# A new hand-written order of the operations on four engines, two merged GpSimd operations and one tile in bf16

## What is computed

```python
xn = _layernorm(x)                       # each row of 128
# branch 1: a complex decaying filter along the 1024 rows, as an FFT convolution
filt = phazor[None, :] ** t * phazor_init[None, :]
conv = ifft(fft(filt, 2 * length) * fft(xn, 2 * length))[:, :length]
y = (conv + last_conv * phazor ** (t + 1)) * gate     # the real part is kept
# branch 2: a gated feed-forward layer in blockwise FP4 (blocks of 16)
gate = fp4_linear(xn, w_gate)            # 128 -> 352
up   = fp4_linear(xn, w_up)              # 128 -> 352
out2 = fp4_linear(silu(gate) * up, w_down)            # 352 -> 128
# fp4_quant_dequant: scale = max|block| / 6, round x / scale to 0, .5, 1, 1.5, 2, 3, 4, 6, times scale
```

## Time and profile before

| | |
|---|---|
| median of 3 runs | 137.35 us (136.39, 139.78, 137.35) |
| the profiled execution | 136.12 us, of which 134.2 us are the span of the instructions |
| busy | DVE 120.5 us (90%), PE 111.9 (83%), POOL 111.0 (83%), ACT 98.9 (74%) |
| mean granted TensorE clock | 0.949 |

### The profile page before, as it was taken

The page is one execution under the profiler, slowest core; times in us unless marked ns, Lnnn a source line. Parts: engine busy times, 40 slices in busy tenths (PEclk is TensorE's granted clock), DMA queues, the critical chain, the costliest instruction groups (busy, mean ns, idle before and its releaser), DMA issues.

```text
span 134.2 us, 2145 instructions
## 1 busy us (share of the span) xinstructions
PE 111.9 (83%) x641; PEld 84.4 (63%) x641; DVE 120.5 (90%) x215; ACT 98.9 (74%) x223; POOL 111.0 (83%) x130
## 2 busy tenths in 40 slices
PE   3603789869377998899899999999999999997993
PEld 3501154536244867677787879686968877787872
DVE  0889999999999999979999999999999999999850
ACT  3869966699983799579897988569776647744541
POOL 4668996999699989999999999999999944982440
PEclk9975799986986999999999999999999999999999
DMA  4990000000000000200020001002000200020111
GB/s 122 280 379 16 0 2 0 0 5 0 0 0 0 5 0 0 78 0 5 0 78 0 0 33 55 0 0 78 0 0 0 83 0 0 0 78 0 67 58 39
DMA packets 2891, 4.90 MB, mean 37 GB/s; under 512 B 448, under 2 KB 832, under 8 KB 2880
## 3 DMA queue, kind: packets, MB, share of 16 engines
q1 hardware_dynamic: 2736, 4.77, 10.4%
q10 hardware_dynamic: 144, 0.00, 0.1%
HBM read 2.67 MB, written 2.10 MB: 36 GB/s over the span
## 4 chain that ended last, share of the span: by engine, by line
POOL 43%; DVE 21%; issue 18%; PE 7%; ACT 6%; DMA 2%; POOLq 1%; DVEq 0%; ACTq 0%
POOL hq L472 9%; POOL y_im L459 6%; POOL y_re L459 6%; POOL u_im L444 5%; POOL u_re L444 5%; POOL xt L416 5%; POOL xt L411 5%; DVE bn L988 4%; POOL xv L406 2%; DMA par<-params_in 2%; ACT xn L629 2%; PE ps_u L853 2%; DVE ps_u L1095 2%; DVE ps_u L1064 1%; DVE ps_u L1060 1%
## 5 line engine op out<-in xcount | busy, mean ns | idle before, releaser
L844 PE MATMUL ps_g<-wg_T,xq_T 128*128 128x352 f32 x64 | 26.8, 502 | 7.3 <-ACT silu L661 5.0
L472 POOL TENSOR_TENSOR hq<-hn,den 128x704 f32<-128x704 bf16 x15 | 20.8, 1390 | 4.3 <-DVE hn L1102 4.3
L904 PE MATMUL ps_o<-wd_T,hq_T 128*128 128x128 f32 x174 | 24.2, 275 | 0.0
L853 PE MATMUL ps_u<-wu_T,xq_T 128*128 128x352 f32 x64 | 23.6, 490 | 0.1
L904 PEld LDWEIGHTS ps_o<-wd_T,hq_T 128*128 128x128 f32 x174 | 22.1, 194 | 0.0
L661 ACT ACTIVATE silu<-ps_g 128x352 f32<-128x352 f32 x32 | 14.8, 461 | 8.4 <-PE ps_g L844 8.1
L844 PEld LDWEIGHTS ps_g<-wg_T,xq_T 128*128 128x128 f32 x64 | 10.3, 193 | 13.2 <-ACT silu L661 8.2
L671 ACT ACTIVATE big<-ps_u 128x704 bf16<-128x704 f32 (+1 forms) x17 | 12.2, 725 | 7.4 <-DVE ps_u L1090 7.4
L667 ACT COPY hq_T<-ps_h 128x384 f32<-128x384 f32 x31 | 14.8, 479 | 3.3 <-PE ps_h L880 3.1
L1095 DVE SCALAR_TENSOR_TENSOR ps_u<-big,ps_u 128x704 f32<-128x704 bf16 (+1 forms) x17 | 14.4, 849 | 1.7 <-ACT big L671 1.4
L880 PE MATMUL ps_h<-ident,hq 128*128 128x128 f32 x93 | 15.6, 276 | 0.1
(11 more groups left out here) (176 smaller groups left out, 260.8 us busy)
## 6 DMA issues: line engine op xcount, KB each, us to landing
x_all<-x_in SPq DMA_DIRECT2D x8, 256.0 KB, 6.0
out<-x_all SPq DMA_DIRECT2D x7, 256.0 KB, 2.0
w_raw<-w_in SPq DMA_DIRECT2D x1, 560.0 KB, 5.5
out<-x_all SPq DMA_DIRECT2D x1, 128.0 KB, 1.7
out<-x_all SPq DMA_DIRECT2D x2, 64.0 KB, 1.6
par<-params_in ACTq DMA_DIRECT2D x1, 3.5 KB, 2.9
```

Source lines behind the costliest of these rows:

```text
L472: pool.tensor_tensor(hq_blocks(q), hn_blocks(q), pair_scales(den[q % 4]), ALU.mult).then_inc(s_hq, 1)
L844: pe.matmul(ps_g[:, 0:I], x_cols(t), wg_T[:, :], start=True, stop=True).then_inc(s_gate, 1)
L853: pe.matmul(slot(q)[:, j, 0:I], x_cols(t), wu_T[:, :], start=True, stop=True).then_inc(s_up, 1)
L904: m = pe.matmul(o, hq_T[t % 3][:, c * P:(c + 1) * P], wd_T[:, c, :], start=False, stop=(c == NCH - 1))
```

## The change

All loops over q and over groups are gone: each of the four engines' blocks is a list of calls, one call for each operation, in a new order. Functions that issued several instructions are cut into one function for each, so that the list can put something between them. On POOL, `u_re` and `u_im` become the halves of one tile `u` of 128 x 2 x 512, likewise `state` and `y`; for groups 2 to 7 one operation makes both halves of `u` (`demodulate_both`), for groups 1 to 6 one makes both halves of `y` (`modulate_both`). Each merged operation waits for both scans of its input and releases both halves at its end. `xbig` is kept in bf16. What is computed, the tiles and the PSUM slots are the same, and so is the number of DVE, ACT and PE operations in the steady part. Cut to what the prediction speaks of:

```diff
-        xbig = [sb(f"xbig{k}", [P, GT]) for k in range(2)]
+        xbig = [sb(f"xbig{k}", [P, GT], BF16) for k in range(2)]
...
+        u = [sb(f"u{k}", [P, 2, GT]) for k in range(2)]
+        state = [sb(f"state{k}", [P, 2, GT]) for k in range(2)]
+        y = [sb(f"y{k}", [P, 2, GT]) for k in range(3)]
...
+        OWN = (0, 1, 2, 3, LAST)
...
+            def demodulate_both(g):
+                pool.wait_ge(s_xnTc, g + 1)
+                pool.wait_ge(s_scan[0], g - 1)
+                pool.wait_ge(s_scan[1], g - 1)
+                pool.tensor_tensor(u[g % 2][:, :, :], xn_T[g % 2][:, :].unsqueeze(1).to_broadcast([P, 2, GT]),
+                                   in_tab[:, :, :], ALU.mult).then_inc(s_u, 2)
+
...
+            def modulate_both(g):
+                pool.wait_ge(s_scan[0], g + 1)
+                pool.wait_ge(s_scan[1], g + 1)
+                if g >= 3:
+                    pool.wait_ge(s_down, TG * (g - 2))
+                pool.tensor_tensor(y[g % 3][:, :, :], state[g % 2][:, :, :], out_tab[:, :, :],
+                                   ALU.mult).then_inc(s_y, 2)
...
-            for q in range(SETTLED, NP):
-                g = q // 2
-                if q % 2 == 0:
-                    modulate_im(g - 1)
-                    if g + 2 < NG:
-                        divide_x(g + 2, 1, 0, GT)
-                    demodulate_im(g)
-                    scale_h(q - 1)
-                    modulate_re(g)
-                else:
-                    if g + 2 < NG:
-                        shift_x(g + 2, 1, 0, GT)
-                        shift_back_x(g + 2, 1, 0, GT)
-                    if q == LAST:
-                        modulate_im(g)
-                    scale_h(q - 1)
-                    if g + 2 < NG:
-                        scale_x(g + 2, 1, 0, GT)
-                    if g + 1 < NG:
-                        demodulate_re(g + 1)
...
+            scale_h(3)
+            shift_x(4)
+            shift_back_x(4)
+
+            scale_h(4)
+            scale_x(4)
+            demodulate_both(3)
+            divide_x(5)
+            modulate_both(2)
+
+            scale_h(5)
+            shift_x(5)
+            shift_back_x(5)
...
-            for q in range(SETTLED, NP):
-                g = q // 2
-                if q < LAST:
-                    silu_tile(2 * q + 2)
-                copy_hT(2 * q - 4)
-                if q % 2 == 0:
-                    copy_out(g - 2)
-                    if g % HALVES:
-                        turn_state(g - 1)
-                    silu_tile(2 * q + 3)
-                    copy_hT(2 * q - 3)
-                    scales(q)
-                    if g + 1 < NG:
-                        copy_xqT(g + 1, 1, 0, GT)
-                    if g + 2 < NG:
...
+            silu_tile(12)
+            normalise(23)
+            big_x(4)
+            big_h(4)
+            silu_tile(13)
+            copy_hT(5)
+            scales_above(5)
+            scales(5)
+            copy_xnT(3)
+            normalise(24)
+            normalise(25)
+            copy_hT(6)
+            normalise(26)
+
...
-                if q < LAST:
-                    turn_h(b)
-                if q >= 4 and q % 2 == 0 and q // 2 + 1 < NG:
-                    turn_xq(q // 2 + 1, 1, 0, GT)
-                if q < LAST:
-                    up_pair(q + 1)
-                if q in (0, 2):
-                    turn_xq(q // 2 + 1, 1, 0, GT)
-                if q + 1 < LAST and (q < SETTLED or q % 2 == 1):
-                    gate_tile(2 * q + 4)
-                if q >= 2:
-                    sum_parts(a, out_cols(a))
-                    sum_down(a, out_cols(a))
-                    sum_parts(b, out_cols(b))
-                    sum_down(b, out_cols(b))
-                if q % 2 == 0 and q // 2 + 1 < NG:
-                    turn_xn(q // 2 + 1)
...
+            up_tile(10)
+            up_tile(11)
+            gate_tile(12)
+            turn_xn(3)
+            turn_h(5)
+            gate_tile(13)
+            sum_parts(4)
+            sum_down(4)
+            sum_parts(5)
+            turn_h(6)
+            sum_down(5)
+            gate_tile(14)
+
+            up_tile(12)
+            up_tile(13)
+            sum_parts(6)
+            turn_h(7)
+            sum_down(6)
+            sum_parts(7)
+            gate_tile(15)
+            turn_xq(4)
+            turn_h(8)
+            sum_down(7)
...
-            for q in range(SETTLED, NP):
-                g = q // 2
-                product(q)
-                shift_h(q - 1, 0, 0, PAIR)
-                shift_back_h(q - 1, 0, 0, PAIR)
-                amax_h(q)
-                if with_x(q):
-                    x_amax((q + 5) // 2, maxima(q)[:, X_COLS])
-                if q % 2 == 0:
-                    scan_re(g, q)
-                if q % 2 == 1 and q < LAST or q == LAST - 1:
-                    scan_im(g, q)
-                if q < LAST:
-                    inverses(q, with_x(q))
-                else:
-                    scales(q, False)
...
+            product(1)
+            amax_h(1)
+            first_x_amax(2)
+            scales(1)
+            first_x_scales(2)
+            inverses(1)
+            first_x_inverses(2)
+            divide_h(1)
+            scan(0, 1, 0)
+            scan(0, 1, 1)
+            shift_h(1)
+
+            product(2)
+            shift_back_h(1)
+            amax_h(2)
+            first_x_amax(3)
+            scales(2)
+            first_x_scales(3)
+            inverses(2)
+            first_x_inverses(3)
+            scan(1, 2, 0)
+
...
+            product(4)
+            shift_h(3)
+            amax_h(4)
+            shift_back_h(3)
+            scan(2, 4, 0)
+            inverses(4)
+
+            product(5)
+            divide_h(4)
+            amax_h(5)
+            pair_x_amax(5)
+            shift_h(4)
+            shift_back_h(4)
+            inverses(5)
+            scan(2, 5, 1)
+            divide_h(5)
+
+            product(6)
+            shift_h(5)
...
+            product(14)
+            shift_h(13)
+            amax_h(14)
+            shift_back_h(13)
+            scan(7, 14, 1)
+            inverses(14)
+            scan(7, 14, 0)
+            divide_h(14)
+
+            product(15)
+            shift_h(14)
+            amax_h(15)
+            shift_back_h(14)
+            scales(15)
+            inverses(15)
```

More of the change, by code:

```diff
@@ new lines, in _ @@
+            divide_h(1)
[11 more added lines that the diff above has]
+            scan(1, 2, 0)
+            product(3)
+            divide_h(2)
+            amax_h(3)
+            pair_x_amax(3)
+            shift_h(2)
+            scales(3)
+            shift_back_h(2)
```

1181 lines of the change are left out of this document (818 added, 363 removed).

## The result

The changed kernel takes 129.84 us (median of 4 runs, 129.22 to 130.58) against 137.69 us for the kernel before on the same chip: the ratio is 0.946, with a 95% interval of 0.936 to 0.957. The forecast was 131.7 us. The direction was right; the time is 1.9 us under the forecast and 0.06 us under 129.9, the lower end of the range. (By the ratio, 0.946 of the 137.35 us that the forecast started from is 129.9, the end itself.) The four executions lie in two clusters some 1.2 us apart, 129.22 and 129.31 us against 130.36 and 130.58; the profiled one is of the longer kind.

A forecast was written before the change was run, and what follows sets the result against it. DVE's queue was taken as the bound. Terms of -2.8 - 1.5 - 1.0 - 0.4 + 0.9 = -4.8 took the profiled 136.12 to 131.3 us; 0.4 added gave 131.7 us, range 129.9 to 136.0.

The forecast's parts named there:

- What bounds the kernel: Whole kernel: DVE's queue from the first product on sets the time, 12.57 us per group, not POOL with 43% of the chain.
- Term 1: DVE's steady part: parting dependent neighbours saves 0.12 to 0.13 us each, 0.48 a group; -2.8 us in all.
- Term 2: DVE's three waits of 0.94, 0.15 and 0.47 us, from 50 to 124 us, go away: -1.5 us.
- Term 5: New wait for the PSUM slot ahead of DVE's product in six odd pairs, 0.15 us each: +0.9 us.
- Term 3: DVE's pairs 0 to 3: nine dependent neighbours parted at 0.12 us, less moments moved there from the head: -1.0 us.
- Term 4: The head, before product(0): three moments come later and divide_w no longer waits for the scales of x: -0.4 us.
- POOL and bf16 at zero: POOL's merged operations and bf16 xbig: savings hidden under DVE, with 0.2 us a group to spare; no gain counted.
- (a): Rival on DVE: start-to-start distances belong to the kinds of instruction, not their order; 134.6 us, chance 8%.
- (b): Rival: PE reaches up_tile of odd pairs late, so DVE waits 0.7 us in six pairs; 135.0 us, chance 12%.
- (c): Rival: DVE's 0.94 us wait for ACT's queue comes back in two or three groups; 134.0 us, chance 13%.
- (d): Rival: POOL's merged 1024-column operations cost 0.9 us more each, and POOL passes DVE; slower at 139.7 us, chance 6%.
- (e): Better case: no wait at the PSUM slot and the whole gain of the head; 130.4 us, chance 6%.

The follow-up runs named there:

- experiment 5: The kernel after with xbig in f32 rather than bf16, u and y still merged: 130.77 us, ratio 0.953 to before.
- experiment 6: The kernel after with u and y made by two operations of 512 columns each, xbig still bf16: 129.40 us, ratio 0.945 to before.
- Experiment 9: The kernel after, unchanged, run once more: 129.90 us, ratio 0.947 to before; its profiled execution took 129.24 us.
- experiment 1: The kernel before with only amax_h moved between shift_h and shift_back_h on DVE, pairs 4 to 15: 138.18 us, ratio 1.014 to before.
- experiment 3: The kernel after with DVE's old order from pair 4 on, other engines keeping the new lists: 138.57 us, ratio 1.016 to before.
- experiment 4: The kernel after with the old lists of TensorE and ACT from pair 4 on: 140.49 us, ratio 1.025 to before.
- experiment 2: The kernel after with shift_back_h right behind shift_h again in even pairs 4 to 14: 129.53 us, ratio 0.950 to before.
- experiment 11: The kernel after with the maxima of x between shift_h and shift_back_h in pairs 5, 7 and 9: 130.01 us, ratio 0.952 to before.

## Why the prediction came out as it did

**What bounds the kernel** was read rightly. DVE's queue set the time before and sets it after, and the chain's 43% for POOL would have led astray: POOL's group was shortened by 0.2 us twice, and taking either back cost the stretch nothing (experiments 5 and 6).

**The sum.** The terms came to -4.8 us. Experiment 9's profile has -6.9 us (129.24 against 136.12), of which the span has -6.8: -4.0 in the stretch, -2.1 in pairs 0 to 3, -0.4 in the head and -0.3 behind product(15). The first profile has -5.8, with its late head. The prediction then put the median 0.4 us above the profiled execution, and in the first runs of after it lay 0.5 below.

**Term 1** (-2.8) was too small. A group fell by 0.42 us net, with the slot's 0.18 in it, so 0.60 rather than 0.48 gross. Of the difference, 0.09 is a thing that no row of before shows for a scan: behind a reciprocal it takes 1.18 us rather than 1.27, in pairs 5, 7, 9, 11 and 14. (In the earlier trace rows a TENSOR_SCALAR behind a reciprocal took 0.14 us; the same one took 0.20 elsewhere in that trace.) Its mechanism, the dependent neighbour, was shown by experiment 1; its worth was not what I made of it.

The prediction took from the Trainium skill, page "VectorE: DVE Perf Modes", section "The DRAIN you can't avoid", a rule by which no order is cheaper than another. That was half of the section. It adds: "A next op that is not held starts earlier". These runs agree with that sentence for an operation whose semaphore is up, with 0.80 us against 0.93 for the same two instructions (experiment 1). The section's other statement, that a semaphore behind each operation costs nothing extra, doesn't hold here where the next operation waits for that semaphore: 0.12 us.

**Term 2** (-1.5) was right: the waits of 0.94, 0.15 and 0.47 us are gone. **Term 5** (+0.9) was right in sum: five odd products wait 0.18 us each, where the prediction had six at 0.15. Product(15) doesn't wait, as a scan and `divide_h` stand between the reciprocal and it. Terms 1, 2 and 5 together: -3.4 forecast, -4.0 measured.

**Term 3** (-1.0) was mis-sized: product(0) to product(4) fell by 1.9 to 2.1 us. The mechanism was right and the count was wrong. DVE has no wait over 0.1 us in these pairs, before or after, so it was not stalls that went. The distances from start to start, before against experiment 9, show 17 parted neighbours where I counted nine, each closer by 0.11 to 0.18 us, 2.2 in all; the other distances give some 0.5. The three moments that moved here cost 0.6 of that again. The prediction left these 0.6 us to term 4, and term 4 doesn't charge them. Two of the 17, in pair 1, before:

```profile
31.95 0.69 DVE L1045 TENSOR_REDUCE ps_u<-xn 128x32 f32<-128x512 f32 x1
32.67 0.19 DVE L1052 TENSOR_SCALAR den_x<-ps_u 128x32 f32<-128x32 f32 x1
```

and in experiment 9:

```profile
31.37 0.68 DVE L1460 TENSOR_REDUCE ps_u<-xn 128x32 f32<-128x512 f32 x1
31.96 0.19 DVE L1498 TENSOR_SCALAR den<-ps_u 128x44 f32<-128x44 f32 x1
32.08 0.19 DVE L1471 TENSOR_SCALAR den_x<-ps_u 128x32 f32<-128x32 f32 x1
32.19 0.42 DVE L1509 RECIPROCAL inv<-den 128x44 f32<-128x44 f32 x1
```

The maxima are followed after 0.59 us rather than 0.72, and `den_x` after 0.11 rather than 0.23 (32.90 in the earlier trace rows).

**Term 4** (-0.4) is right in experiment 9 (-0.41, product(0) at 21.29) and has the wrong sign in the first profile (+0.51), where the lower level of TensorE's clock held the head up. The prediction had no case for that. What bounds the head has changed too: before, product(0) followed the moments without a wait; now the moments are done at 20.4 us and it waits for `up_tile`. No term stood for the tail; of its -0.2 to -0.3 us, before had a wait of 0.47 ahead of the `shift_h` at 127.05, and after has none there.

**POOL and bf16 at zero** was right for the steady part, and for the reason given: DVE covers it, by some 0.2 us a group (POOL's idle 0.20 and 0.33 us in after). The values differ: bf16 did act (1.17 us; I took 1.28, with 1.06 as the bound). What the prediction missed is that the two are cover for each other: with both taken back the stretch grows by 1.0 us. It also took bf16 as hidden in the head, where POOL's chain to the first `xv` is not hidden, but that is worth 0.1 us.

**The rivals.** (a) fell with experiment 1. (b) and (c) did not come about: TensorE is busy 9.72 to 10.00 of 10 us and still reaches the slot in time, and no wait of the old kind is left in the stretch. (d) fell by the 2.37 us of the merged operations. (e), at 6% and 130.4 us, is nearest to the measured time, though not for its reasons: the wait at the slot is there. That the lower end of the range was so nearly right is luck in part: it was set from (e), and the time came there by terms 1 and 3 being larger. What the forecast lacked was a case in which both are, and so the range was too tight below.

**What it did not see at all** is how the parts hang together. It adds up terms as if each could be had alone. Experiments 1, 3 and 4 show that a part of the new order, run with old lists on the other engines, or the other way round, has the other sign.

## What to carry to other kernels

An order written out for several queues is one thing: to find what it is worth, change it on all engines that hand work to each other, since half of a good order can be slower than none. Before parting two dependent neighbours on DVE (0.12 us here), look at when the buffer that the second one frees is wanted, and whether the instruction that moves up has its input; in the three places tried in the steady part (experiments 1, 2 and 11) half of the gain or more than all of it was given back there. In pairs 0 to 3, where DVE had no wait before or after, the parted neighbours gave their 0.12 us each in full. And two edits that each measure nothing may be cover for one another: take both back before either is called free.
